# Sharing the open expert blocks between both token halves, with GpSimd's fills and third batch moved into the attention loop

## What is computed

```python
x = x + _L0_xattn_ref(ctx_1024, _layernorm(x), ...)      # memory compression
x = x + _L0_ffn_ref(_layernorm(x), ...)                  # shared expert + top 2 of 8 experts
x = x + _L1_xattn_ref(_layernorm(x), ctx_1024, ...)      # 16 heads, 64 context rows
x = x + _L1_ffn_ref(_layernorm(x), ...)                  # top 2 of 8 experts
```

## Time and profile before

| | |
|---|---|
| median of three executions | 808.31 us |
| the profiled execution's own time | 811.32 us |
| its span, first to last instruction | 809.4 us |
| mean granted TensorE clock | 0.98 |
| PE busy | 749.4 us (93%) |
| first layer's slots, first half | 137 to 188 us |
| first layer's slots, second half | 199 to 255 us |
| attention's loop | 257 to about 500 us |

### The profile page before, as it was taken

One profiled execution on the slowest core, in us unless ns is written; L12 is line 12 of the kernel. 1 busy time (PEld: TensorE's weight loads), 2 busy tenths in 40 slices (PEclk: granted clock), 3 DMA queues, 4 the chain that ended last, 5 costly groups with the idle time before them and its releaser, 6 DMA issues.

```text
span 809.4 us, 16195 instructions
## 1 busy us (share of the span) xinstructions
PE 749.4 (93%) x4633; PEld 652.7 (81%) x4633; DVE 533.4 (66%) x1422; ACT 492.5 (61%) x1379; POOL 433.1 (54%) x400
## 2 busy tenths in 40 slices
PE   5799998999988699999999999799999999999995
PEld 4545746777766589999998998689999999999984
DVE  4777867753773688888889979776534344366455
ACT  3336845765765788887787797365554454445441
POOL 4000565766677668887646878345642454333251
PEclk9889999999997999999999999999999999999998
DMA  8999997997998952852800634814434434564447
GB/s 241 352 282 317 332 304 260 288 294 210 233 267 197 321 154 41 238 110 33 273 3 2 224 116 139 268 59 138 143 121 140 151 106 156 183 208 166 145 150 267
DMA packets 128745, 154.47 MB, mean 191 GB/s; under 512 B 10875, under 2 KB 118550, under 8 KB 127638
## 3 DMA queue, kind: packets, MB, share of 16 engines
q1 hardware_dynamic: 102896, 112.55, 45.1%
q0 software_dynamic: 18624, 34.29, 16.0%
q10 hardware_dynamic: 7142, 6.59, 2.5%
HBM read 77.39 MB, written 76.00 MB: 190 GB/s over the span
## 4 chain that ended last, share of the span: by engine, by line
PE 63%; DVE 11%; DMA 7%; POOL 6%; issue 5%; ACT 4%; DVEq 2%; SPq 1%; ACTq 0%; POOLq 0%
PE psum L864 20%; PE psum L1157 8%; PE psum L1181 8%; PE psum L1253 6%; PE psum L1258 6%; PE psum L1254 6%; POOL X L721 3%; PE psum L1269 3%; ACT pr L1566 2%; PE psum L1167 2%; POOL xs_dram L762 2%; DMA fx<-xs_dram 2%; PE psum L1232 2%; DMA w_sb<-in_L_ffn_W_dram 2%; DMA X<-yl_dram,slots_y 1%
## 5 line engine op out<-in xcount | busy, mean ns | idle before, releaser
L774 POOL DMA_INDIRECT yk_dram<-ys,L x52 | 54.4, 1046 | 129.9 <-ACT ys L1658 129.5
L721 POOL DMA_INDIRECT X<-yl_dram,slots_y x64 | 102.0, 1594 | 29.8 <-issue 14.2
L1566 ACT ACTIVATE pr<-psum,nmx 128x64 f32<-128x64 f32 x512 | 108.5, 363 | 15.0 <-DVE nmx L2331 14.6
L693 POOL DMA_INDIRECT xs_dram<-N,slots x64 | 65.5, 1023 | 92.1 <-DVEq L1960 62.2
L1253 PE MATMUL psum<-whi,xTh 128*128 x284 | 103.7, 365 | 2.4 <-ACT xTh L1620 1.5
L2428 DVE TENSOR_TENSOR hs<-psum,hs 128x384 f32<-128x384 f32 x71 | 39.7, 560 | 88.6 <-PE psum L1258 81.7
L1254 PE MATMUL psum<-wlo,xTh 128*128 x284 | 95.4, 336 | 0.0
L762 POOL DMA_INDIRECT xs_dram<-N,slots x64 | 69.6, 1088 | 35.7 <-ACT ys L1658 19.2
L1258 PE MATMUL psum<-whi,xTl 128*128 x284 | 73.5, 339 | 3.7 <-DVE xTl L2451 3.7
L754 POOL TENSOR_TENSOR pr<-pr,sm 128x1024 f32<-128x1024 f32 x30 | 57.2, 1907 | 18.0 <-DVE sm L2338 16.5
L1650 ACT ACTIVATE hs<-psum 128x384 f32<-128x384 f32 x71 | 34.9, 491 | 50.5 <-PE psum L1258 46.7
(11 more groups left out here) (374 smaller groups left out, 2056.3 us busy)
## 6 DMA issues: line engine op xcount, KB each, us to landing
fx<-xs_dram SPq DMA_DIRECT2D x78, 130.0 KB, 3.7
yl_dram<-fy SPq DMA_DIRECT2D x78, 128.0 KB
xs_dram<-fill SPq DMA_DIRECT2D x4, 2340.0 KB, 16.5
xs<-xs_dram SPq DMA_DIRECT2D x71, 130.0 KB, 3.1
wlo<-in_L_ffn_W_dram SPq DMA_DIRECT2D x4, 1536.0 KB, 9.5
xs_dram<-cz SPq DMA_DIRECT2D x1, 5070.0 KB, 22.8
xs_dram<-cz SPq DMA_DIRECT2D x7, 650.0 KB, 6.6
X<-in_x_dram SPq DMA_DIRECT2D x4, 1024.0 KB, 12.1
```

Of the source, the lines that this page charges most:

```text
L693: po.indirect_dma_start(XS, bass.IndirectOffsetOnAxis(ap=slot[k][:, t:t + 1], axis=0), N0[:, t, :], None).then_inc(s[done], 16)
L721: po.indirect_dma_start(X[:, t, :], None, YL[b // 2], bass.IndirectOffsetOnAxis(ap=slot_y[k][:, t:t + 1], axis=0), compute_op=ALU.add).the ...
L774: po.indirect_dma_start(YK, bass.IndirectOffsetOnAxis(ap=yid[:, j:j + 1], axis=0), ys[j % YB], None).then_inc(s[f"y_out{j % YB}"], 16)
L1566: last = act(pr[b][:, S * h:S * h + S], bank[2 * b + h // 8][:, S * (h % 8):S * (h % 8) + S], ACT.Exp, bias=nmx[:, h:h + 1])
```

## The change

The first layer's list gets 71 slots. The first 25 (`LF`) hold only full blocks of the first half. Slots 25 to 32 and on are open: an expert's rows of the first half that do not fill a block lie in an open slot, and the second half's rows of that expert go on in it. So the loop of the first half has 25 slots, the one of the second 46 (`ENDS`), and the first half's results are complete with slot 39 (`LO` = 40), in the second half's loop. `places` is rewritten with separate paths for g = 0 and 1. The table `eid` of slots 33 to 70 is no longer written there but by `open_experts` in DVE's loop at slots 5 and 7. The pacing constant `SLOTS` goes from 5 to 3. The statistics of batch 0 move to the loop's last seven slots for its first four tiles (`STATS`, `NORMED`), and for the other four to `between(0)` and `between(1)` of the attention. The second-choice fetches wait for half a batch each (semaphores `l_ga`/`l_gh` and `l_gb`/`l_gd`). On POOL the six fetches of batch 2 ahead of the loop and the writing of `fill` and of row numbers between them leave their place: all 32 fetches of batches 2 and 3 are in the loop, one each at n = 0 and 1, then two each up to n = 16, and `filler()` runs at n = 6.

```diff
-LS = 2 * LT + E - 1
-LA = LG * LS
+LF = 2 * LT - E + 1
+LR = LF + E
+LO = 2 * LT + E
+LA = 2 * TILES + E - 1
+ENDS = (0, LF, LA)
+HALF = BT // 2
+STATS = {LA - 7: (0, 2), LA - 6: (2, 4)}
+NORMED = {LA - 5: (0, 1), LA - 4: (2, 3), LA - 3: (4,), LA - 2: (5,), LA - 1: (6, 7)}
-BREAK, SLOTS = 4, 5
-HEAD = 3
+BREAK, SLOTS = 4, 3
...
-                first, last = LS * g, LS * g + LS
+                first, last = ENDS[g], ENDS[g + 1]
...
             def routed_done(g):
 
                 po.wait_ge(s["l_xu"], LQ * (g + 1))
                 for b in range(YB):
-                    po.wait_ge(s[f"ys_out{b}"], routed_out(b, LS * (g + 1)))
+                    po.wait_ge(s[f"ys_out{b}"], routed_out(b, (LO, LA)[g]))
...
             routed_done(1)
-            collect(2, 0, 2 * BT, 2 * BT + HEAD)
-            po.memset(fill[:, :, 0:X0 - 1], 0.0).then_inc(s["consts"], 1)
...
-            numbers(0)
-            collect(2, 0, 2 * BT + HEAD, 2 * BT + 2 * HEAD)
-            late = [(b, k, t) for b in (2, 3) for k in range(2) for t in range(b * BT, b * BT + BT)][2 * HEAD:]
+            late = [(b, k, t) for b in (2, 3) for k in range(2) for t in range(b * BT, b * BT + BT)]
+
+            def filler():
+
+                po.memset(fill[:, :, 0:X0 - 1], 0.0).then_inc(s["consts"], 1)
+                po.memset(fill[:, :, X0:XW - 1], 0.0).then_inc(s["consts"], 1)
+                for side in (X0 - 1, XW - 1):
+                    po.iota(fill[:, :, side], ...).then_inc(s["consts"], 1)
+                numbers(0)
...
+                if n == 6:
+                    filler()
                 for m in ROWED.get(n, ()):
                     rows_in(m)
-                for _ in range(1 if n < 4 else 2):
+                for _ in range(1 if n < 2 else 2):
                     if late:
                         b_, k_, t_ = late.pop(0)
                         collect(b_, k_, t_, t_ + 1)
...
+                    if j in (5, 7):
+                        open_experts((j - 5) // 2)
-                    if j == LS // 2:
+                    if j == LF // 2:
                         combined(1)
...
             def routed_norm(b, half):
 
-                if half == 0:
-                    ve.wait_ge(s["l_gb"], 16 * BT * (b + 1))
+                ve.wait_ge(s[("l_gb", "l_gd")[half]], 16 * HALF * (b + 1))
...
                 def between(n):
+                    if n == 0:
+                        routed_norm(0, 1)
+                        chain(0, ((HALF, BT),), 1)
+                    if n == 1:
+                        chain(1, ((HALF, BT),), 1)
+                        ve.drain()
+                        chain(2, ((HALF, BT),), 1)
                     if n in (1, 2):
                         routed_norm(1, n - 1)
```

More of the change, by code:

```diff
@@ L734, in _ @@
             for b in range(2):
-                for k in range(2):
-                    collect(b, k, b * BT, b * BT + BT)
+                collect(b, 0, b * BT, b * BT + BT)
+                for t in (b * BT, b * BT + HALF):
+                    collect(b, 1, t, t + HALF)
             def numbers(g):
@@ L1465, in routed @@
             def routed(g):
-                first, last_ = LS * g, LS * g + LS
+                first, last_ = ENDS[g], ENDS[g + 1]
                 def silu(j):
@@ L1894, in scores, with places @@
                             row_stats(N0, t, t + BT)
-            def places(n, cols, prefix, totals, tot_, inc_, cm, heads, base, nslots, at, t0, done):
+            def places(g):
+                n, cols = LT, E * LT
                 e3 = "p (e t) -> p e t"
+                prefix, totals = (bank[4][:, 256 + 128 * k:256 + 128 * k + cols] for k in range(2))
+                tot_, inc_ = (tc_[:, cols * k:cols * k + cols] for k in range(2))
                 ta_, tb_ = ta[:, 0:cols], tb[:, 0:cols]
+                ta3, tb3 = ta_.rearrange(e3, e=E), tb_.rearrange(e3, e=E)
+                last_t = inc_.rearrange(e3, e=E)[:, :, n - 1:n]
+                last = last_t.rearrange("p e a -> p (e a)")
+                past, delta, start, grow, upto, jump = (ta[:, cols + 32 + E * k:cols + 32 + E * k + E] for k in range(6))
+                nslots, at = (LR, LA - LR)[g], (0, LR)[g]
+                number, e_at = slotno[:, at:at + nslots], eid_f[:, 0:nslots]
+                behind, part = (tb[:, cols + 64 * k:cols + 64 * k + nslots] for k in range(2))
+                cm = wk12[:, 0:nslots * E].rearrange("p (j e) -> p j e", e=E)
@@ L1925, in places, with open_experts @@
                 ve.drain()
-                ts(slots[:, :, t0:t0 + n], hot2[:, :, 0:n], float(base), None, ALU.add)
-                nc.vector.tensor_copy(slots_y[:, :, t0:t0 + n], hot2[:, :, 0:n])
+                nc.vector.tensor_copy(slots[:, :, n * g:n * g + n], hot2[:, :, 0:n])
+                if g == 0:
+                    nc.vector.tensor_copy(slots_y[:, :, 0:n], hot2[:, :, 0:n])
                 ve.drain()
-                if done:
-                    ve.sem_inc(s[done], 1)
+            def open_experts(half):
+                cols, nslots = E * LT, LA - LR
+                upto = ta[:, cols + 32 + 4 * E:cols + 32 + 5 * E]
+                behind, part = (tb[:, cols + 64 * k:cols + 64 * k + nslots] for k in range(2))
+                cm = wk12[:, 0:nslots * E].rearrange("p (j e) -> p j e", e=E)
+                e_at = eid_f[:, 0:nslots]
+                ve.drain()
+                if half == 0:
+                    ts(behind, slotno[:, LR:LA], opened[:, 0:1], None, ALU.subtract)
+                    nc.vector.tensor_copy(slots_y[:, :, LT:TILES], hot2[:, :, 0:LT])
+                    ve.drain()
+                    ts(part, behind, 0.0, float(E), ALU.is_lt, ALU.mult)
+                    tt(cm, bc(behind, E), rep(upto, nslots), ALU.is_ge)
+                else:
+                    stt(part, behind, 0.0, part, ALU.min, ALU.add)
+                    nc.vector.tensor_reduce(e_at, cm, AX.X, ALU.add)
+                    ve.drain()
+                    stt(eid[:, LR:LA], e_at, float(E - 1), part, ALU.min, ALU.add)
+                    ve.drain()
             def choose(g):
@@ L1976, in routed @@
                     ve.drain()
-                for j in range(LS * g, LS * g + LS):
-                    if j == LS * g or j % 4 == 0:
+                first = ENDS[g]
+                for j in range(first, ENDS[g + 1]):
+                    if j == first or j % 4 == 0:
                         experts_of, loaded = four_experts(mybir.EngineType.DVE, j), j
@@ L2013, in first_norm @@
                 elif part < 7:
[L2014 removed]
+                    ln_newton(HALF)
                 else:
```

137 lines of the change are left out of this document (85 added, 52 removed).

## The result

The changed kernel takes 833.45 us, median of four executions (827.31 to 835.95), beside 808.9 for the kernel before (807.04 to 812.59): a ratio of 1.029, 95% interval 1.025 to 1.033. It is slower by 24.6 us. The forecast was 828 with the range 815 to 839. The profiled execution has a span of 834.1 us against 809.4, 24.7 more, so the traces can be set against each other without a correction.

The account below looks back on a forecast made before the run. TensorE, busy 93%, was taken as the bound, so waits on the way to it cost their length. Slots +1, start +1, fills +11 and last fetches +7 made +20 on 811.32, 831.3; less 3.0 for the median, 828, range 815 to 839.

Parts of the forecast that it names:

- The fills: Attention loop, n = 9: araw queues on SP behind two late fills and ACT waits 11.2 us; +11 us, bounds 5 and 17.
- Rival B: araw does not queue behind the fills, only the last fetches cost: 817 us; chance 0.10.
- The last fetches: Attention loop, n = 17: DVE waits for the last late fetch, issued at n = 16; +7 us, 4 to 9.
- rival E: Waits add up worse: PE's clock drops at both stops, fetches stretch beside the fills; +30, 838 us; chance 0.12.
- The slots: First layer's slot stage: seven slots saved, but longer places and a bare wait for rows; +1 us, bounds -4 and +5.
- The start of the attention: n = 0 and 1: DVE's some sixteen small steps for batch 0's other half norm; +1 us, 0 to 4.
- A: Rival: the slots' gain shows and nothing waits, 799 us; chance 0.04.
- D: Rival: neither fills nor last fetches cost, slots and start alone, 810 us; chance 0.04.
- signs named ahead: Fill issues about 318 us; idle ACT 9 to 13, DVE 8 to 10, PE 5 to 8 us; first transposes near 192.
- C: Rival: the fills cost, the last fetches don't, 821 us; chance 0.14.

Follow-up runs that it names:

- fills early: The changed kernel with GpSimd writing the fill rows ahead of the attention loop again, late fetches as changed: ratio 1.0157 to the kernel before.
- fills behind `araw`: The changed kernel with fills still in n = 6, but SP issuing araw of the third batch ahead of the two fill DMAs: ratio 1.0204.
- the late fills alone in the kernel before: The kernel before with only GpSimd's writing of the fill rows moved into n = 6 of the attention loop: ratio 1.0156.
- chain spread: Changed kernel, fills early, two fetches from n = 0, vraw behind the slot loads, last part of batch 0's second-half norm chain in n = 2: ratio 1.0023.
- batch 1 later: Changed kernel, fills ahead of the loop, two fetches from n = 0, batch 1's statistics in n = 2 and 3 instead of 1 and 2: ratio 1.0018.
- the kernel before with vraw moved: The kernel before with the load of vraw behind the first loads of the second half's slots: ratio 1.0014.
- two fetches from the start: The changed kernel with fills ahead of the loop and two late fetches in every iteration from n = 0: ratio 1.0012.
- vraw behind: Changed kernel, fills ahead of the loop, two fetches from n = 0, vraw's load behind the second half's first seven slot loads: ratio 0.9997.
- the changed kernel beside it: The changed kernel itself, run again for comparison on the same chip as three follow-up kernels: ratio 1.0271.

## Why the prediction was right

**The fills, +11 against +12.0.** Each link of the forecast stands in the trace. SP's fills were said to go out at 317.9; they went at 319.77. `araw` was to land at 341.0; ACT starts on it at 343.81, with the loop 2.7 us later than before. The two fills landed 11.7 and 20.9 us after their issue, at about 331.5 and 341, and `araw`, 20.6 after its own, at 343.8: in the order of issue. ACT's wait was 11.15 us (forecast 11.2), TensorE's 9.14 (9.5). Mis-sized is the clock behind the stop: the step is 12.0 us longer and 9.14 of it are the idle time, so 2.9 are lost to slow work and late restart, where I added 1.5. That `araw` is late because it stands behind the fills was tested three ways: fills early, fills behind `araw`, and the late fills alone in the kernel before. Rival B is out. Whether the load is held by the data ahead of it or by its own slow issue (9.56 us) these runs can't part.

**The last fetches, +7 against +9.5.** The last issue was said to be at 392.7, with 14.5 us of earlier delay 407.2; it is at 407.31. The landing of 5.4 to 8 us was 7.9. DVE's wait was put at 8.8 to 10.3 and was 10.94, TensorE's part of it at 7, and its idle time was 6.99. What the sum left out is again the clock: 2.5 us of half speed after the stop. I had it in rival E alone. The evidence was in the earlier trace rows, and I used it for the longer stop only; the trace has the low clock behind the gaps of 5.35, 6.99 and 9.14 us alike.

**The slots, +1 against -0.5.** `places` was to move the first send by 2.4 us; it moved by 0.3, from the earlier trace rows's 137.49 to 137.82. Here a step failed. DVE does release the sends, but the 1.7 us of `places(0)` were wrongly added: ahead of `choose(1)` DVE waits 4.36 us for TensorE in both traces and begins it at 122.23 before and 122.11 after, so nothing of `places(0)` gets through. `places(1)` itself, put at +0.7, went from 5.23 to 5.68 us. The last send went out at 180.24 instead of the forecast 182.4, TensorE's wait for rows was 5.35 us (6.8), and the first transposes began at 188.65 instead of 192.2. Of these 3.5 us 2 were lost again, with the first slots at the low clock: the second half's first store is at 194.15 (195.7). That most of what seven slots save is eaten up by loads that are now bare holds for this trace; the others put the gain of the slots at up to some 4 us (above).

**The start of the attention, +1 against +3.2.** I had priced DVE's sixteen small steps. The trace has DVE waiting 2.55 us in n = 1 for batch 1's fetch and TensorE waiting 3.58 for `prl`. The first two rows are the issue of the fetch that DVE needs, the 28th, and the last of the small steps in n = 1:

```profile
265.61 1.56 POOL L728 DMA_INDIRECT X<-yl_dram,slots_y  x1 [0.30 <-issue]
271.30 0.17 DVE L2164 TENSOR_SCALAR nshift<-nshift 128x4 f32<-128x4 f32 x1
274.02 1.41 DVE L1781 BATCH_NORM_STATS2 xstats<-X 128x6 f32<-128x256 f32 x4 [2.55 <-DMA X<-yl_dram,slots_y]
280.45 2.08 PE L1193 MATMUL psum<-Vh,prl 128*128 128x256 f32 x8 [3.58 <-DVE prl L2429]
```

The cause I named is not the one. In n = 1 the small steps end at 271.47, before the fetch is there, so they only shorten DVE's wait. The wait comes from POOL's row of fetches: it begins at 214.93, behind slot 39, and the fetches follow at 1.85 us or a little more. I had asked only when the 32nd lands. The same numbers give 273.7 for the 28th (217.3 + 27 x 1.89 + 5.4), which is the one that n = 1 needs, and 274.02 was measured. This would also explain why an earlier `logits(0)` brings little: the row starts with slot 39 and takes its 50 us. Behind the wait comes slow work: TensorE's next product takes 2.08 us instead of 1.12. The two kernels that moved small steps (chain spread) or the wait (batch 1 later) gained nothing, but both have the fills and fetches early; in the second POOL is late with `scale`, while in the changed kernel POOL itself waits 1.70 us for DVE ahead of `scale` at 286.62. The start of the changed kernel as it stands was not tested by a run of its own, so this cause is read from its trace and argued. How large the term is stays uncertain: n = 0 to 10 took 79.15 us in one trace of the changed kernel and 81.16 in the other.

**Step 22, +2.1, not forecast.** It took 9.2 to 9.7 us in seven of the fourteen traces and 10.4 to 11.8 in the other seven, with and without the stops ahead of it (10.7 in the kernel before with vraw moved). The changed kernel itself has 11.22 in one trace and 9.65 in the other, so the +2.1 of the table is not shown to be the change's. I can't say what decides between them.

Taken together the sum of +20 was short by 4.7 us: 3.5 at the two stops, nearly all of it the clock behind them, 2.2 at the start and 2.1 in step 22, against 1.5 to the good in the slots, 1.1 at the end and 0.4 in the loop's other steps.

The result lies inside the range and just inside the forecast's own stretch (822 to 834). That it came so near owes something to luck, as the small terms partly cancel. (The chances given for below 815, A, D and half of B, add up to 0.13, not 0.12.) Of the signs named ahead, ACT's wait, TensorE's wait for rows and SP's issues came as said; DVE's wait in n = 17 was 0.9 us over its 8 to 10, and the first transposes were 3.4 us earlier than the 192 named. Of rival E the clock came true, at both stops, and the last fetch did take 7.9 us beside a fill, which the sum allowed for. A, C (fetches hidden) and D are out by the waits of ACT and DVE.

None of the kernels beats the one before. The fills ahead of the loop with two fetches from the start, with or without vraw behind, come level with it.

## What to carry to other kernels

When a step is moved down an engine's program, look for the semaphore it raises and then for everything queued behind whoever waits for it: here four small writes of POOL put two large DMAs, 21 us to the landing of the second, ahead of a load that ACT needed. When fetches are postponed, work out for every reader when the fetch it needs lands, not for the last alone. At two fetches a step of 7.4 us POOL had some 0.5 us left (two fetches from the start, from 305 to 378 us), and at three the step grew to 8.6, so they can't be caught up later. And price each stop of TensorE as the idle time plus the half-speed work after it, which was 2.5 to 2.9 us for stops of 7 to 9.

## What the hardware showed that I had not expected

A DMA's issue can itself be slow: SP took 9.56 us to issue `araw` behind the two fills, 9.55 in the changed kernel beside it, and 0.32 us with nothing large in front of it (fills behind araw, 311.83). So SP, which issues the DMAs, was held up there. It is not so for every DMA behind a fill: `vraw`, issued next at 332.98 with the second fill still on its way, took 1.10 us, and the store of X behind the third fill 12.47. What decides this the traces don't show.

A DVE operation on 128x8 numbers took 4.19 us, where its like take 0.17 (the kernel with batch 1 later, at 283.32). It ended at 287.51. POOL's `split_low` and `scale` ran beside it, and `scale` ended at 287.47. In the kernel with two fetches from the start one of 1.36 us at 284.32 ended at 285.68, and `scale` at 285.64:

```profile
284.32 1.36 DVE L2110 TENSOR_TENSOR tatb<-xstats 128x8 f32<-128x8 f32 x1
283.15 2.49 POOL L762 TENSOR_TENSOR pr<-pr,sm 128x1024 f32<-128x1024 f32 x1
```

The Trainium skill, SBUF — State Buffer, section Who interferes with whom, says that a VectorE instruction with two SBUF inputs contends with a GpSimd instruction that reads SBUF, and that the order of issue decides which of the two blocks. The row at 284.32 agrees with it: the DVE operation has two inputs, starts behind `scale` and ends 0.04 us after it. The one at 283.32 has two inputs and ends with `scale` too, but by the record it starts ahead of `split_low` (283.76) and `scale` (284.98), so it agrees in its end only. There TensorE waited for POOL and not for DVE, so no time can be put down to it here.
